# A graph network with routed experts: eight banks for the weighted sum, and three index scatters laid beside other stages

## The reference

```python
# layer 1, typed graph attention: one softmax for each destination node and edge type
att = (q[dst] * key_e).sum(-1) * rel_pri[etype] / sqrt_dk
alpha = exp(att - segment_max) / segment_sum(...)
hmsg = segment_sum(alpha[..., None] * val_e, seg)
t = hmsg.sum(1) / jnp.maximum(present.sum(1, keepdims=True), 1.0)
out1 = typed_linear(t, node_type, Wa, ba) * a + x * (1.0 - a)
# layer 2: eight experts, 256 -> 1024 -> 256, the two best of each node
out2 = (weights[:, :, None] * sel).sum(axis=1)
# layer 3, six steps of a gated graph network on the same edges
msg = segment_sum(h[src], dst)
# layer 4: attention on another graph (32768 edges and self loops) picks two of four experts
```

## Time and profile before

| | us |
|---|---|
| median of 3 runs | 8556.6 |
| lowest, highest | 8552.79, 8558.91 |
| the profiled execution | 8561.61 |
| its span in the profile | 8559.7 |

### The profile page before, as it was taken

How to read it: one execution, slowest core, us unless ns; L and a number is a source line. 1 busy time by engine, 2 the same in 40 slices (tenths; PEclk the granted TensorE clock), 3 DMA queues, 4 the chain that set the end, 5 groups by cost and what they waited for, 6 DMA issues and landing times. The chain is left out here.

```text
span 8559.7 us, 87812 instructions
## 1 busy us (share of the span) xinstructions
PE 6177.8 (72%) x21499; PEld 3748.1 (44%) x21507; DVE 3598.2 (42%) x8884; ACT 1407.1 (16%) x2363; POOL 3435.4 (40%) x4286
## 2 busy tenths in 40 slices
PE   6668658457725667496464699999999999555645
PEld 1123224234412333485121466666666666443545
DVE  6822961156666665111995322222212222333622
ACT  0011001011110001121341122222222222111011
POOL 0766867756606770673773472000000000265022
PEclk9778889766756668798786799999999999555568
DMA  2022002123302330464002211111111111000045
GB/s 96 2 67 71 0 20 78 49 71 90 90 7 81 86 86 8 139 195 142 2 1 98 65 54 51 48 52 46 50 50 54 45 56 54 7 7 6 0 126 174
DMA packets 420073, 519.09 MB, mean 61 GB/s; under 512 B 174610, under 2 KB 341016, under 8 KB 419864
## 3 DMA queue, kind: packets, MB, share of 16 engines
q1 hardware_dynamic: 304024, 376.73, 14.0%
q0 software_dynamic: 115840, 139.64, 6.6%
HBM read 389.40 MB, written 126.18 MB: 60 GB/s over the span
## 5 line engine op out<-in xcount | busy, mean ns | idle before, releaser
L911 POOL COPY gs_from_ids<-gat_src_row 128x8 uint16 (+1 forms) x80 | 15.9, 199 | 2188.7 <-SPq L129 2188.4
L2221 PE MATMUL gg_p_all<-gg_edges,nodes 128*128 128x384 f32 (+2 forms) x2700 | 797.1, 455 | 0.6 <-DVE nodes L2368 0.6
L2221 PE MATMUL gg_p_all<-gg_edges,gg_other 128*128 128x384 f32 (+2 forms) x2700 | 797.3, 455 | 0.0
L2379 DVE SCALAR_TENSOR_TENSOR gg_gates<-gg_into,gg_per_edge,gg_p_all 128x384 f32<-128x384 uint16 (+2 forms) x216 | 124.3, 575 | 1343.1 <-PE gg_p_all L2244 1343.1
L2221 PEld LDWEIGHTS gg_p_all<-gg_edges,nodes 128*128 128x128 f32 x2700 | 502.3, 190 | 287.1 <-issue 1.0
L2221 PEld LDWEIGHTS gg_p_all<-gg_edges,gg_other 128*128 128x128 f32 x2700 | 502.4, 190 | 285.9
L1302 PE MATMUL ha_p_sum<-ha_weighted,ha_hot 128*128 128x258 f32 x832 | 389.8, 631 | 253.9 <-DVE sums L1263 243.0
L399 POOL DMA_INDIRECT cell_sorted<-cell_scatter_what,cell_scatter_at x392 | 437.3, 1116 | 170.2 <-issue 87.4
L2057 PE MATMUL ce_p_cell<-ce_hot_at,ce_hot_src 128*128 128x512 f16 (+1 forms) x1280 | 283.3, 354 | 295.3 <-DVE ce_hot_src L2017 143.9
L916 POOL DMA_INDIRECT ha_values<-v_table,ha_value_rows x416 | 407.4, 979 | 182.9 <-issue 93.5
L916 POOL DMA_INDIRECT hs_keys<-k_table,hs_key_rows x416 | 396.9, 954 | 183.1 <-issue 89.7
(11 more groups left out here) (502 smaller groups left out, 10844.0 us busy)
## 6 DMA issues: line engine op xcount, KB each, us to landing
gg_packed<-cell_counts SPq DMA_DIRECT2D x150, 800.0 KB, 4.3
e_w<-in_L_ffn_W_dram SPq DMA_DIRECT2D x64, 1024.0 KB
e_w<-in_L_ffn_W_dram SPq DMA_DIRECT2D x56, 512.0 KB
k_table<-hp_kr SPq DMA_DIRECT2D x25, 1024.0 KB
v_table<-hp_kr SPq DMA_DIRECT2D x25, 1024.0 KB
cell_counts<-cell_acc SPq DMA_DIRECT2D x5, 4000.0 KB
slots<-clear_zeros SPq DMA_DIRECT2D x15, 1024.0 KB
e_rows<-slots SPq DMA_DIRECT2D x60, 256.0 KB, 4.9
```

The source lines that it names most:

```text
L2221: mm = pe.matmul(p_all[:, half, 0:n], rows[:, t, half * P:(half + 1) * P], edges[:, turn % 2, t, 0:n], start=t == 0, stop=t == tiles - 1)
L2379: dve.scalar_tensor_tensor(out=to, in0=into[:, own], scalar=per_edge[:, i * halves + k:i * halves + k + 1], in1=p_all[:, bank, 0:n], op0=A ...
```

## The change

1. `hgt_sum` gets eight PSUM banks in place of two. Chunk b of a round of eight has a bank of its own, and PE waits for the sum of chunk c-8 rather than c-2. DVE adds in the same order as before, from the bank that belongs to the chunk.
2. The second part of the cell scatter (columns 136 to 391) is spread: 88 columns (136 to 223) in one block with `segment_softmax`, 80 (224 to 303) in one block with `hgt_update`, and 88 (304 to 391) beside the experts.
3. Gat's first scatter is split: its first 176 columns follow the cells beside the experts, the other 112 stay beside `sum_cells`.

```diff
-    p_sum = ctx.enter_context(nc.psum_tensor("ha_p_sum", [P, 2, 512], F32))
+    p_sum = ctx.enter_context(nc.psum_tensor("ha_p_sum", [P, SLOTS, 512], F32))
...
-                dve.tensor_tensor(to, to, p_sum[:, b % 2:b % 2 + 1, 0:wide], ALU.add).then_inc(added, 1)
+                dve.tensor_tensor(to, to, p_sum[:, at_slot + b:at_slot + b + 1, 0:wide], ALU.add).then_inc(added, 1)
...
-                if not (first and b < 2):
-                    pe.wait_ge(added, c - 1)
-                pe.matmul(p_sum[:, b % 2, 0:wide], hot[:, b, :], weighted[:, b, :],
+                if not first:
+                    pe.wait_ge(added, c + (1 - SLOTS))
+                pe.matmul(p_sum[:, b, 0:wide], hot[:, b, :], weighted[:, b, :],
...
-        segment_softmax(g, hgt, att, 0.0)
+        with together(g):
+            scatter_cells(g, cell, 136, 224)
+            segment_softmax(g, hgt, att, 0.0)
...
-        hgt_update(g, ins, sums, y, type_hot, x)
+        with together(g):
+            scatter_cells(g, cell, 224, 304)
+            hgt_update(g, ins, sums, y, type_hot, x)
...
         with together(g):
-            scatter_cells(g, cell, 136)
+            scatter_cells(g, cell, 304)
+            scatter_edges(g, gat, 0, 0, 176)
             routed_experts(g, "e0", slots, made, owners, ins["L0_ffn_W1"], ins["L0_ffn_b1"], ins["L0_ffn_W2"],
...
             sum_cells(g, cell, acc)
-            scatter_edges(g, gat, 0)
+            scatter_edges(g, gat, 0, 176)
```

More of the change, by code:

```diff
@@ L1254, in _, with add_batch @@
         dve.wait_ge(begun, 3)
-        def add_batch(c, first):
+        def add_batch(c, at_slot, first):
             at = load_tiles(g, mybir.EngineType.DVE, e, c)
@@ L1281, in body @@
                 if not (first and h == 0):
-                    add_batch(c - HALF, first and h == 1)
+                    add_batch(c - HALF, (1 - h) * HALF, first and h == 1)
         led(dve, n // SLOTS, body)
-        add_batch(n - HALF, False)
+        add_batch(n - HALF, HALF, False)
         dve.wait_ge(added, n)
```

## The result

| | before | after |
|---|---|---|
| median of 5 runs, us | 8556.6 | 8513.28 |
| lowest, highest | 8552.79, 8561.93 | 8509.7, 8518.46 |
| span of the profiled execution | 8559.7 | 8511.6 |

What follows compares the result with a forecast made beforehand. POOL was taken to bound `hgt_sum` and the end of `sum_cells`, PE the experts and update. Terms -1 - 37 + 5 + 1 + 1 = -31 us from the 8556.6 median gave 8526, 8-in-10 range 8498 to 8549.

Steps and rivals of the forecast that it cites:

- its own sign: Forecast called wrong if POOL's `hgt_sum` batch differs from 6.06 us by over 0.15, or softmax grows by over 15 us.
- The bounds of each block: POOL bounds `hgt_sum` and the end of `sum_cells`, PE the experts and update; softmax and update have no POOL instruction.
- Eight banks: In `hgt_sum`: removes DVE's 114.6 us wait for PE, but DVE then waits for gathers; -1 us.
- I take no change: In `hgt_sum`: the one-hot's shift within POOL's batch counted as nothing, between ends of -28 and +61 us.
- The sum runs at the pace of the scores: Rival: in `hgt_sum` the earlier one-hot clears POOL's copy and gather, 28 us fewer, total 8499; 15%.
- The slower rival: In `hgt_sum`: the one-hot starts just ahead of the last gather's read, holding it 0.6 us; +61 us, 8587; 5%.
- `sum_cells`: With 112 columns beside it, its end becomes DVE's: 24 us there plus 14 from faster pairs, taken as -37 us.
- The softmax: 88 scatter columns beside it, 87 counted as hidden; block about +5 us, DVE perhaps +1 us.
- The update: 80 scatter columns beside its 126 us, cover with nothing to spare; 0 to +3, taken as +1 us.
- The experts: 264 columns in place of 256, POOL done at about 3921, cover of 74 us; 0.
- The small blocks between the update and the experts: Blocks between update and experts; forecast change 0.
- The terms other than the banks: `sum_cells` -37, softmax +5 and DVE there +1, update +1, experts 0 us.

Runs made afterwards that it cites:

- Run 6: Kernel before, two banks, one-hots made for the first eight chunks only and reused, so results differ from the reference; 8745.76 us against 8762.34, single execution.
- run 1: Kernel before with the eight banks of `hgt_sum` alone, all scatters as before; 8760.24 us against 8766.51, ratio 0.9989.
- run 3: Changed kernel with the two banks of before, so the moved scatters alone; 8723.12 us, ratio 0.9953 to the kernel before.
- Run 5: Changed kernel, but in `hgt_sum` DVE makes a batch's one-hot behind its four products; 8729.72 us against 8762.34 for the kernel before, ratio 0.9954.
- run 8: Changed kernel with the one-hot between third and fourth product, and 80 and 72 columns in softmax and update; 8585.06 us, ratio 0.9939 to the kernel before.
- run 7: Changed kernel itself, measured again on another chip; 8589.6 us against 8638.28 for the kernel before, ratio 0.9944.

## Why the prediction was right and where it was not

The forecast had the direction and the larger part. Between the two profiled executions it is 31 us against 48 measured, and of the 17 us that are missing the banks are 17, the scatters 3, and the router's projection takes 3 back. By the medians it is 31 against 43, since the profiled execution before lies 5 us above its median. By its own sign it was wrong in one place: POOL's batch in `hgt_sum` was to stay within 0.15 us of 6.06, and came to 5.89.

- **The bounds of each block** were read rightly: `sum_cells` ended by POOL's scatter, `hgt_sum` by POOL's batch, and the waits for PE off the path. Run 6 shows the last: waits of 70.2 us, and a block as short as with eight banks.
- **Eight banks: the mis-sized term.** The failed step is "I take no change". The term was -1 and measured -18.3, or -13.9 between runs 1 and 3. The mechanism was named and the one-hot's place worked out: the one-hot would come 0.5 us earlier, about 0.15 us behind the start of the last DMA. Over some 90 batches from 2640 to 3180 us its start lies 0.69 us behind that DMA's start in the median before, and 0.22 after. What was missing was the last inference, that at 0.22 us it is clear of both sides. A DMA that has started is not held (only 4 of the 92 batches had one held by the one-hot), and the one-hot ends before the copy or just after its start. Before, 66 of 89 copies began within a one-hot, up to 0.68 us ahead of its end, and lasted 0.46 us in the mean; after, 43 of 92 did, all of them in its last 0.25 us, and lasted 0.22. "The sum runs at the pace of the scores" was the nearest rival, with 15%. It came two thirds of the way: 5.89 us against 5.79 in `hgt_scores` and 6.06 before. The price could have been had from the rows: the copies take 380 ns here and 211 in the scores, 0.17 us in each of 104 batches or 18 us, which is what comes back if the one-hot ends as the copy begins. What is left of the 28 us is the other part, DMAs and copies that meet the products: 130 DMAs that began within one (L1277) lasted 1.00 us in the mean, 48 such copies 0.28. Of the 92 us that DVE no longer waits for PE, the forecast put about 100 into waits for gathers; these grew by 41.5, and DVE's waits from one sum to the next, 22 us before and 64 after, took as much.
- **The slower rival** (the one-hot ahead of the last DMA's start, +61 us) didn't happen. Run 5 shows that it was the right kind of fear: there a DMA starts within the one-hot in 61 of 90 batches, mostly the second. It costs 0.21 us a batch and not 0.6, since a DMA held longest loses 0.5, and those that start within 0.02 us of the one-hot lose nothing.
- **`sum_cells`: right.** -40.1 for -37: 26.5 at the end (I took 24, with a barrier of 3 us; it was 0.94) and 13.6 in the pairs (14). POOL was done at 4284.4, where 4292 less 7 for the earlier start was forecast.
- **The softmax: right in length, with two errors that cancel.** The count was 87 columns by 5 us before DVE's end; 88 were done 198.4 us after the block's start, and the scans and the reciprocal did as said. But the time from the last column to the next block was 9.5 us and not 4.7, because POOL's DRAIN took 7.24 us where it takes 2.51 in the block of the earlier trace rows. It costs 3.9 us of the 4.9, since after ACT's last copy the next block begins in about 1 us when POOL is done (run 8). And DVE's chain grew by 0.9 us. So the loss came not from columns that didn't fit, but from the tail.
- **The update: right in length, wrong in the tail** in the same way. POOL's last column ended at 3331.53, and the next block's first instruction stands at 3340.80, 9.3 us later, with a DRAIN of 6.59 us between; DVE's last instruction had ended at 3338.26.
- **The experts: right**, 0.4 us. POOL was done at 3910.7, where 3921 was forecast.
- **The small blocks between the update and the experts: a term put at nothing** that measured +2.8. It is the router's projection (`project_nodes`), a block bound by PE whose code the change doesn't touch: 29.2 us before, 32.3 after. The stretch holds it, before and after (fields as above, 0.56 and 0.50 are the granted clock):

```profile
3379.00:3409.00 30.00, 27.86 (x150) 27.71 (x150) 4.51 (x7) 3.88 (x7) 0.00 (x0) 0.56 0.01 1
3369.00:3401.00 32.00, 30.96 (x150) 30.76 (x150) 4.52 (x7) 3.88 (x7) 0.00 (x0) 0.50 0.01 1
```

Before, TensorE has its upper clock level (granted 1.0, 2.4 GHz) from 3382.7 to 3386.1 us, and eight products there take 0.96 us; at the lower level (0.50, 1.2 GHz) they take 1.71. After, the whole block runs at the lower level. The block takes 29.2 us in the three profiles with two banks (before, runs 3 and 6) and 32.3 to 33.9 in the eight with four or eight, so this loss goes with the banks and makes their net gain about 15 us. What in `hgt_sum` decides it isn't shown.

The terms other than the banks were forecast at -30 and came to about -33 without those 2.8 us.

The Trainium skill, page "SBUF — State Buffer", section "Who interferes with whom", infers that a DVE instruction with two SBUF inputs doesn't stop descriptor generation. The traces disagree: an indirect DMA that met a scan lasted 7.76 us, and one that met the one-hot 1.42. Its rule that an instruction with at most one SBUF input, outside the two-port modes, doesn't contend agrees with the 0.95 to 0.98 us beside the reciprocal.

## What to carry to other kernels

Where one engine's instruction can hold up another's, read where in the other's cycle it falls: an edit that only removes waits on an engine with spare time can still pay, because it moves that instruction, and its price is what the one now hit loses. Compute the place from a trace of the order that you will have, and not from one in which the instruction still stands elsewhere: 0.2 us decided between a gain and a loss. Work laid under a block must be done ahead of that block's end by its whole tail, and the tail has to be read for the very length of scatter that you will have: here some 3 to 12 us, by the number of columns, as the rows on the DRAIN below add up.

## What the runs showed of the hardware

- A POOL indirect DMA that begins while DVE runs an instruction with two SBUF inputs is held; one that began before it, or within 0.02 us of its start, is not. In run 5, 61 DMAs began within a one-hot of 0.69 us: those at 0.00 to 0.02 us from its start lasted 0.95 us, those at 0.03 either 0.95 or 1.47, those at 0.05 to 0.37 between 1.47 and 1.13, the shorter the later. In run 8 it is 0.97 and 1.50 on the first DMA, with the same edge. A held DMA ends some 0.8 us behind the DVE instruction, in the softmax too (2470.78 + 7.76 = 2478.54, the scan's end 2477.75).
- A copy of POOL is held as well, and ends 0.04 us behind the DVE instruction. It hasn't the margin at the start: two copies of the kernel before that began with a one-hot, within 0.01 us, lasted 0.73 us.
- The control for the two SBUF inputs stands in the same loop: 184 DMAs of the changed kernel began within a sum (L1263, 0.42 us, one input in SBUF and one in PSUM) and lasted 0.94 to 0.96 us. But two inputs aren't the only case: in the softmax a DMA that began within a TENSOR_SCALAR over one tensor (L1151) lasted 2.24 us.
- Beside DVE's reciprocal of 20.95 us POOL's DMAs ran at their full pace.
- The other way round, DVE's pair of `sum_cells`, its own work unchanged, takes 1.40 us beside POOL's scatter and 1.32 without it.
- The time from a scatter's last column to the next block is some 1.4 us until POOL's waits are over, then POOL's DRAIN, then 0.8 to 1.1 us. The DRAIN goes by the number of columns of that scatter: 2.02 us for 24 columns, 4.64 for 56, 5.94 for 72, 6.59 for 80, 7.24 for 88, 9.21 for 112, that is 0.65 us for each eight; then 1.20 for 120, 2.51 for 136 (2.79 in the first scatter of the program), 1.70 for 232, 3.65 for 256, 6.27 for 288. Where several profiles have the same scatter, they agree to 0.01 us, on up to four chips (72, 120 and the like stand in one or two profiles only), and 80 columns gave 6.59 in the update and in the softmax alike. Why it grows so and falls back past 112 is open, and no run was made to test it.
- The same kernel before took 8557 us on one chip, 8638 on another and 8762 and 8767 on two more. `hgt_scores` took 609, 652 and 688 us on the first, the second and the last of these (after, run 7, run 3), and the experts 477 to 478 us on the first two and 532 to 560 on the others. A gain of a few us is to be sought in a block's length, not in the total.
